# First attention of a two-layer kernel: keys placed alike in every tile, one weight tile a head, weights broadcast from SBUF to SBUF

## The chip, the core and the metric

One core of a Trainium2 chip runs the whole program in one launch. The metric is the device time in microseconds (us). The engines are named as in the profile: PE is the matmul engine (PEld its weight loads), DVE the vector engine, ACT the scalar engine, POOL GpSimd, SP the sync engine, which here only issues DMAs (its queue is SPq).

## The reference, cut to what matters

Two batches of 1,024 tokens go through a layer 0 (attention, then a soft mixture of experts) and a layer 1 (causal attention, then a routed one). Only layer 0's attention is touched. It has 16 query heads over 4 groups of keys and values, head size 64, and its softmax runs in each chunk of 64 keys apart:

```
kc = k.reshape(B, NH, C, SPLIT, HD)        # C = 16 chunks of SPLIT = 64 keys
vc = v.reshape(B, NH, C, SPLIT, HD)
scores = jnp.einsum('bhqd,bhckd->bhcqk', q, kc) * scale
w = jax.nn.softmax(scores.astype(jnp.float32), axis=-1).astype(q.dtype)
chunk_out = jnp.einsum('bhcqk,bhckd->bhcqd', w, vc)
sum_w = w.sum(axis=-1, keepdims=True)
combined = (chunk_out * sum_w).sum(axis=2)
total = sum_w.sum(axis=2)
out = combined / (total + 1e-09)
```

So each exponential is multiplied by a weight that depends on its query and on its key's chunk: 16 x 1,024 weights a head.

## The kernel before, in words

Each engine has its program written out by hand; within a batch the 16 heads are unrolled, and a hardware loop runs over the two batches. Semaphores alone tie the engines together. The batch's attention of layer 0 lasts from about 22 to 534 us, the second one from about 1,105 to 1,620 us.

Queries, keys and values are projected from `att_in` (128 features x 1,024 tokens) by `project_q` (L677), `project_k` (L682) and `project_v` (L688). Tile t holds keys 128t to 128t+127, so it holds chunks 2t and 2t+1: partitions 0 to 63 are one chunk, 64 to 127 the other.

For head i, in `head0(i)`, PE goes through eight steps t:

- `scores(i, t)` (L771, L776): the scores of key tile t against all queries, in two parts (high and low halves of fp32 numbers), 128 keys x 1,024 queries. ACT takes the exponential into `EE` (L1502).
- `maxima(i + 1, ...)` (L750): scores of the next head, queries on partitions, 512 keys at once; DVE reduces each to 8 chunk maxima `mx` (L1919). PE may be only two of these ahead of DVE (banks 5 and 6). They are transposed at the head's end (`turn_maxima`, L757) and are needed by the next head's scores.
- `values0` (L814) of the heads before, two tiles at every odd t, once DVE has multiplied `EE` by the weights (`weigh`, L1948).
- at t = 3 and 5 one projection for the next group (`project_next`).
- at t = 1 `turn_normalisers(i - 1)` (L803).

After the eight steps come `chunk_sums(i)` (L786), the next-but-one head's first two maxima, and `turn_sums(i)` (L796).

The weights of head i are made in this chain: `chunk_sums` sums `EE` over each chunk by a matmul with a 0/1 matrix, four column tiles of 32 at once, 16 matmuls of 512 columns (fp32, so each is two passes in the trace: 32 records a head); ACT copies the sums to `S_sb` (L1482, 128 x 512); `turn_sums` turns them by four transposes; DVE's `normaliser` and `normaliser_parts` (L1928 to L1940) work on 128 numbers a partition; `turn_normalisers` turns them back by four transposes; ACT copies them to `r_rows` (L1477, 128 x 512). Then SP writes four pieces of 16 KB to the DRAM tensor `weight_rows` (`weight_rows_out`, L503), waits for them, and fetches for each key tile two rows, each broadcast over 64 partitions, into a ring of four tiles that lies in `V1` (`weight_tiles_in`, L515: 16 DMAs of 256 KB a head). Each tile's refill waits until DVE has used the tile four before it (`p3_mul`). DVE weighs head i's tiles 0 to 3 at t = 5 and 7 of head i+1, and tiles 4 to 7 at t = 1 and 3 of head i+2.

After head 15 there are no scores: DVE makes head 15's normalisers, weighs tiles 4 to 7 of head 14 and the eight of head 15, and PE does the last values with the output projection (L881) between them.

Of the kernel before, what the change touches and what calls it, by code (L numbers as in the profile page):

```python
# [12 lines left out]
AX = mybir.AxisListType.X  # L13
ds = bass.ds


P = 128
# [18 lines left out]
CQ = NC // 2  # L36
# [3 lines left out]
              "eps_row": NT, "chunk": 4 * 32}  # L40
# [26 lines left out]
def layer_program(nc, A, out, sorted_in, sorted_out, weight_rows):  # L67
    ctx = ExitStack()
    with ctx:
# [16 lines left out]
        chunk_sum = const("chunk").rearrange("p (a c) -> p a c", a=4)  # L86
# [53 lines left out]
        weight_ring = [v[:, :, :].rearrange("p t d -> p (t d)").rearrange("p (o q) -> p o q", o=2) for v in V1]  # L140
# [15 lines left out]
        S_sb = own0[:, 2 * BANK:3 * BANK]  # L156
        r0 = sb("r0", [P, 4, 4, CQ])
        sw = sb("sw", [P, 4, 4, CQ])
        r1 = sb("r1", [P, 4, 4, CQ])
        tot = sb("tot", [P, 4, 2])  # L160
        rp = sb("rp", [P, 4, 4, 32])
        r_rows = sb("r_rows", [P, BANK])
# [200 lines left out]
        wr_in = sem("wr_in")  # L363
        wt_in = [sem(f"wt_in{i}") for i in range(4)]
# [84 lines left out]
        def _(sp):  # L449
# [33 lines left out]
            with sp.Fori(0, NB) as b:  # L483
                for L in range(2):
                    if L == 0:
# [11 lines left out]
                        def weight_rows_out(i):  # L497

                            sp.wait_ge(s_rr, b * HEADS + i + 1)
                            sp.sem_inc(s_held, 1)  # L500
                            for j in range(4):
                                half, odd = divmod(j, 2)
                                sp.dma_start(weight_rows[i % 2, odd * CQ:(odd + 1) * CQ, half * BANK:(half + 1) * BANK],  # L503
                                             r_rows[32 * j:32 * j + CQ, :]).then_inc(wr_in, 16)

                        def weight_tiles_in(i, a):

                            for odd in range(2):
                                t = 2 * a + odd
                                if i >= 1 or t >= 4:  # L510
                                    sp.wait_ge(p3_mul, 1 + (b * HEADS + i) * NT + t - 3)
                                    sp.sem_inc(s_held, 1)
# [8 lines left out]
                        for i in range(HEADS):  # L521
                            weight_rows_out(i)
                            sp.wait_ge(wr_in, (b * HEADS + i + 1) * 64)
                            sp.sem_inc(s_held, 1)
                            for a in range(4):
                                if a == 3 and i % GH == GH - 1 and i // GH + 2 < GROUPS:
                                    next_group(i // GH + 2)
                                weight_tiles_in(i, a)
# [102 lines left out]
        def _(pe):  # L631
# [31 lines left out]
            def attention0(b):  # L663
# [3 lines left out]
                krows = HD + NC  # L667
                h0 = b * HEADS
# [68 lines left out]
                def maxima(i, units):  # L737
# [3 lines left out]
                    for x in units:  # L741
# [8 lines left out]
                        pe.matmul(banks(5 + x % 2, BANK), Q_HIGH[u][:, t * P:(t + 1) * P], KA[g % 2][:, half * BANK:(half + 1) * BANK],  # L750
# [29 lines left out]
                def chunk_sums(i, a):  # L780

                    pe.wait_ge(s["p2_exp"], 1 + (h0 + i) * NT + 2 * a + 2)
                    for half in range(2):
                        for odd in range(2):
# [4 lines left out]
                    if a == 3:  # L789
# [9 lines left out]
                def turn_normalisers(i):  # L799

                    pe.wait_ge(rp_out, h0 + i + 1)
                    for k in range(4):
# [17 lines left out]
                def head0(i):  # L820
# [20 lines left out]
                    for a in range(4):  # L841
                        chunk_sums(i, a)
# [552 lines left out]
        def _(act):  # L1395
# [36 lines left out]
            def attention0(b):  # L1432
# [12 lines left out]
                def high_k(g, half, bank):  # L1445

                    act.wait_ge(s["proj_k"], 1 + 2 * (g0 + g) + half + 1)
                    act.activation(KA[g % 2][:, half * BANK:(half + 1) * BANK], banks(bank, BANK),
# [23 lines left out]
                def normalisers(i):  # L1472

                    act.wait_ge(rb_ps, h0 + i + 1)
                    if i >= 1:
                        act.wait_ge(wr_in, (h0 + i) * 64)
                    act.activation(r_rows[:, :], banks(4, BANK), ACT.Copy).then_inc(s_rr, 1)  # L1477
# [1107 lines left out]
```

## Time and profile before

| | |
|---|---|
| median of 3 runs | 2207.07 us (2201.11 to 2214.0) |
| the profiled execution's own time | 2210.59 us |
| its span, first to last instruction | 2208.5 us |
| PE busy | 1976.8 us, 90% of the span |
| DVE busy | 1440.1 us, 65% |
| ACT busy | 980.7 us, 44% |
| moved by DMA | 187.99 MB |

The span is the profiled execution seen from its first instruction to its last; 2.1 us of its time lie outside. PE's busy time counts matmuls that overlap once.

### The profile page before, as it was taken

The page shows a single profiled execution, that of the slowest core. Times are in us where ns is not written, and L with a number is a line of the kernel's source. Part 1 is how long each engine was busy: PE and PEld are TensorE (multiplying, and loading weights), DVE is VectorE, ACT ScalarE, POOL GpSimd, SP SyncE. Part 2 cuts the span into 40 slices and gives each one's busy share as a digit, 9 for nine tenths or more (in the row PEclk, how much of TensorE's full clock was granted, in tenths as well). Part 3 has the DMA queues.
Part 4 walks back from the last instruction along what each step waited for, and adds up shares of the span by engine and source line. Part 5 has one row for each costly group of instructions (what it writes and reads, how often), then busy time and mean ns, then how long its engine had stood idle before and what let it go on. Part 6 is the DMA issues. An engine that isn't in the chain of part 4 may idle for free.

```text
span 2208.5 us, 32078 instructions
## 1 busy us (share of the span) xinstructions
PE 1976.8 (90%) x10106; PEld 1193.3 (54%) x10106; DVE 1440.1 (65%) x2492; ACT 980.7 (44%) x1377; POOL 586.5 (27%) x549
## 2 busy tenths in 40 slices
PE   6899999996997999998888999999979889999985
PEld 4444444444784655556644444444448755655554
DVE  7677788865327777753467887778561377777443
ACT  3444454441224666662334444444413246656422
POOL 0000000000101798884120000000010047897921
PEclk7999999998887999998879999999979879999987
DMA  2366665567000000000516565656750000000024
GB/s 94 84 154 160 155 149 141 139 161 237 24 1 10 2 10 6 1 1 30 163 39 154 141 146 141 146 141 151 182 198 1 1 10 10 1 6 1 1 79 135
DMA packets 84846, 187.99 MB, mean 85 GB/s; under 512 B 17697, under 2 KB 46754, under 8 KB 83106
## 3 DMA queue, kind: packets, MB, share of 16 engines
q1 hardware_dynamic: 83650, 183.76, 32.8%
q0 software_dynamic: 1024, 2.10, 0.3%
q8 instruction: 88, 1.44, 0.3%
q14 instruction: 84, 0.69, 0.1%
HBM read 178.47 MB, written 8.91 MB: 85 GB/s over the span
## 4 chain that ended last, share of the span: by engine, by line
PE 67%; DVE 14%; issue 9%; ACT 3%; DMA 3%; POOL 2%; SPq 1%; DVEq 0%; another core or an unknown queue 0%; POOLq 0%; ACTq 0%
PE PS L814 10%; PE PS L786 5%; PE PS L750 5%; PE PS L986 4%; PE PS L926 4%; PE PS L966 3%; DVE mx L1919 3%; PE PS L881 3%; PE PS L969 3%; PE PS L1159 3%; PE PS L771 3%; PE PS L776 3%; PE PS L1218 2%; DMA V<-weight_rows 2%; POOL Esum L2463 2%
## 5 line engine op out<-in xcount | busy, mean ns | idle before, releaser
L1919 DVE TENSOR_REDUCE mx<-PS 128x8 f32<-128x512 f32 x512 | 329.6, 686 | 178.7 <-PE PS L750 164.0
L2463 POOL TENSOR_TENSOR Esum<-Esum,EE 128x512 f32<-128x512 f32 (+3 forms) x320 | 341.3, 1094 | 15.5 <-POOL Esum L2463 10.5
L1948 DVE TENSOR_TENSOR EE<-EE,V 128x1024 f32<-128x1024 f32 x256 | 303.1, 1219 | 45.3 <-DMA V<-weight_rows 44.7
L1502 ACT ACTIVATE EE<-PS 128x1024 f32<-128x1024 f32 x256 | 259.9, 1024 | 142.7 <-PE PS L776 141.2
L2052 DVE TENSOR_REDUCE mrow<-PS 128x1 f32<-128x512 f32 (+3 forms) x384 | 204.1, 552 | 99.1 <-PE PS L929 69.9
L2405 POOL TENSOR_TENSOR QA<-hT,QA 128x512 fp32r<-128x512 f32 x2 | 2.6, 1282 | 996.5 <-ACT hT L1690 996.5
L814 PE MATMUL PS<-EE,Vlater 128*64 128x512 f32 x1024 | 250.5, 609 | 9.4 <-ACT U L1468 8.3
L750 PE MATMUL PS<-KA,QA 128*128 128x512 f32 x512 | 204.1, 454 | 31.8 <-DVE mx L1919 25.8
L1586 ACT ACTIVATE EE<-PS 128x1024 f32<-128x1024 f32 (+2 forms) x192 | 138.1, 739 | 121.4 <-PE PS L969 118.7
L771 PE MATMUL PS<-QA,KA 128*128 128x512 f32 x512 | 185.1, 443 | 0.0
L750 PEld LDWEIGHTS PS<-KA,QA 128*128 128x128 f32 x512 | 97.8, 196 | 130.3 <-DVE mx L1919 88.4
L776 PE MATMUL PS<-QB,KB 80*128 80x512 f32 x512 | 163.1, 400 | 0.0
L986 PE MATMUL PS<-EE,V 128*64 128x512 f32 (+3 forms) x640 | 131.2, 522 | 0.0
L2077 DVE COPY_PREDICATED EE<-consts,F 128x256 f32<-128x256 int32 x96 | 95.3, 992 | 47.9 <-ACT EE L1586 47.8
L814 PEld LDWEIGHTS PS<-EE,Vlater 128*64 128x64 f32 x1024 | 61.8, 136 | 115.3 <-issue 92.4
L786 PE MATMUL PS<-EE,consts 128*32 128x512 f32 x1024 | 116.5, 595 | 0.8 <-DVE QA L1896 0.8
L771 PEld LDWEIGHTS PS<-QA,KA 128*128 128x128 f32 x512 | 91.9, 192 | 42.6 <-issue 26.8
L776 PEld LDWEIGHTS PS<-QB,KB 80*128 80x128 f32 x512 | 98.1, 192 | 22.3
L926 PE MATMUL PS<-KA,QA 128*128 128x512 f32 (+1 forms) x192 | 91.1, 475 | 19.2 <-DVE mrow L2052 12.3
L2454 POOL TENSOR_TENSOR Esum<-F,consts 128x1024 f32<-128x1024 f32 x32 | 62.2, 1965 | 93.5 <-PE PS L1010 62.4
L926 PE MATMUL PS<-KC,QC 128*128 128x512 f32 (+1 forms) x192 | 84.4, 440 | 0.6
L926 PEld LDWEIGHTS PS<-KA,QA 128*128 128x128 f32 x192 | 38.3, 199 | 72.4 <-DVE mrow L2052 50.1
(321 smaller groups left out, 3373.6 us busy)
## 6 DMA issues: line engine op xcount, KB each, us to landing
V<-weight_rows SPq DMA_DIRECT2D x512, 256.0 KB, 5.4
EE<-in_w SPq DMA_DIRECT2D x48, 192.0 KB, 2.7
V<-in_Wg SPq DMA_DIRECT2D x4, 1024.0 KB, 6.4
EE<-in_Wu SPq DMA_DIRECT2D x4, 1024.0 KB, 11.8
EE<-in_Wd SPq DMA_DIRECT2D x4, 1024.0 KB, 13.5
sorted_out<-U SPq DMA_DIRECT2D x12, 256.0 KB, 3.1
wo<-in_wo SPq DMA_DIRECT2D x5, 512.0 KB, 4.4
wq_s<-in_wq SPq DMA_DIRECT2D x17, 128.0 KB, 2.8
```

Of the source, the lines that this page charges most:

```text
L750: pe.matmul(banks(5 + x % 2, BANK), Q_HIGH[u][:, t * P:(t + 1) * P], KA[g % 2][:, half * BANK:(half + 1) * BANK], start=True, stop=True).t ...
L771: pe.matmul(banks(own, hi - lo, lo), KA[g % 2][:, t * P:(t + 1) * P], Q_HIGH[u][:, lo:hi], start=True, stop=False)
L776: mm = pe.matmul(banks(own, hi - lo, lo), KB[g % 2][0:krows, t * P:(t + 1) * P], Q_LOW[u][0:krows, lo:hi], start=False, stop=True)
L786: mm = pe.matmul(PS[32 * j:32 * j + 32, 4 * BANK:5 * BANK], chunk_sum[:, a, :], EE[i % 2][:, 2 * a + odd, half * BANK:(half + 1) * BANK], ...
L814: mm = pe.matmul(PS[HD * half:HD * half + HD, 7 * BANK:8 * BANK], V0[i // GH % 2][:, t, :], EE[i % 2][:, t, half * BANK:(half + 1) * BANK] ...
L926: mm = pe.matmul(banks(4 + h, hi - lo), M1[h][p % 2][:, t * P:(t + 1) * P], S1[h][p % 2][:, lo:hi], start=True, stop=not own)
L986: mm = pe.matmul(PS[HD * h:HD * h + HD, 6 * BANK + lo:6 * BANK + hi], V1[g % 2][:, t, at:at + HD], e_tile(t)[:, h, lo - t * P:hi - t * P], ...
L1502: act.activation(EE[i % 2][:, t, :], banks(2 * (t % 2)), ACT.Exp, scale=QSCALE).then_inc(s["p2_exp"], 1)
L1919: dve.tensor_reduce(mx[:, t, half * 8:half * 8 + 8], banks(5 + x % 2, BANK).rearrange("p (c k) -> p c k", c=8), AX, ALU.max).then_inc(s["p ...
L1948: dve.tensor_tensor(EE[i % 2][:, t, :], EE[i % 2][:, t, :], weight_ring[a % 2][:, odd, :], ALU.mult).then_inc(p3_mul, 1)
L2052: dve.tensor_reduce(mrow1[:, h, t, half:half + 1], banks(4 + h, width), AX, ALU.max).then_inc(s["mx_red"], 1)
L2463: ins = pool.tensor_tensor(Esum[:, h, lo:hi], Esum[:, h, lo:hi], e_tile(t)[:, h, lo - t * P:hi - t * P], ALU.add)
```

## The change

Key k*8 + t now sits in tile t at partition k. So partition p of every tile belongs to chunk p // 8, and one 128 x 1,024 tile of weights serves all eight tiles of a head. What follows from it:

- `project_k` and `project_v` read `att_in` through the view `by_place`, that is with a step of eight fp32 elements (32 bytes) between neighbours; V as the stationary operand, K as the moving one. The copies of K are written in runs of 64.
- `maxima` takes 64 keys of each of the eight tiles, so its moving operand is eight runs of 64; DVE's reduction (now L1912) takes for each chunk eight runs of eight columns of PSUM, where it took 64 neighbours.
- `chunk_sums` has the same 0/1 matrix for all tiles. Each key tile needs four matmuls of 256 columns: 32 matmuls of 256 a head (64 records), where there were 16 of 512.
- All 16 chunk rows of a quarter of the queries lie together, so `S_sb`, the transposed sums and `r_rows` are 256 columns wide, and `turn_sums` and `turn_normalisers` need two transposes each. The normalisers are still 128 numbers a partition.
- SP issues four DMAs a head, from `r_rows` straight into one of two tiles in `V1`, each of 128 KB, repeating each of 16 source rows over 8 partitions. There is no DRAM scratch, no wait for it, and no ring. `weigh` waits for all four.

```diff
-                        def weight_rows_out(i):
+                        def weights_in(i):
                             sp.wait_ge(s_rr, b * HEADS + i + 1)
                             sp.sem_inc(s_held, 1)
+                            if i >= 2:
+                                sp.wait_ge(p3_mul, 1 + (b * HEADS + i - 1) * NT)
+                                sp.sem_inc(s_held, 1)
                             for j in range(4):
-                                half, odd = divmod(j, 2)
-                                sp.dma_start(weight_rows[i % 2, odd * CQ:(odd + 1) * CQ, half * BANK:(half + 1) * BANK],
-                                             r_rows[32 * j:32 * j + CQ, :]).then_inc(wr_in, 16)
-                        def weight_tiles_in(i, a):
...
-                                for k in range(2):
-                                    row = weight_rows[i % 2, odd * CQ + 2 * a + k, :]
-                                    sp.dma_start(weight_ring[a % 2][HD * k:HD * k + HD, odd, :],
-                                                 row.partition_broadcast(HD)).then_inc(wt_in[t % 4], 16)
+                                rows = r_rows[32 * j:32 * j + NC, :]
+                                sp.dma_start(weights[i % 2][:, j * QUARTER:(j + 1) * QUARTER],
+                                             rows.unsqueeze(1).to_broadcast([NC, CP, QUARTER])).then_inc(wt_in, 16)
...
+                by_place = x_in[:, :].rearrange("p (k t) -> p t k", t=NT)
...
-                    pe.matmul(banks(bank, BANK), wk_s[:, 0, :], x_in[:, half * BANK:(half + 1) * BANK],
+                    pe.matmul(banks(bank, BANK), wk_s[:, 0, :], by_place[:, :, half * HD:(half + 1) * HD],
...
-                        mm = pe.matmul(banks(bank, HD, t * HD), x_in[:, t * P:(t + 1) * P], wv_s[:, 0:HD],
+                        mm = pe.matmul(banks(bank, HD, t * HD), by_place[:, t, :], wv_s[:, 0:HD],
...
-                        pe.matmul(banks(5 + x % 2, BANK), Q_HIGH[u][:, t * P:(t + 1) * P], KA[g % 2][:, half * BANK:(half + 1) * BANK],
+                        keys = KA[g % 2][:, :].rearrange("p (t k) -> p t k", t=NT)[:, :, half * HD:(half + 1) * HD]
+                        pe.matmul(banks(5 + x % 2, BANK), Q_HIGH[u][:, t * P:(t + 1) * P], keys,
...
-                def chunk_sums(i, a):
-                    pe.wait_ge(s["p2_exp"], 1 + (h0 + i) * NT + 2 * a + 2)
-                    for half in range(2):
-                        for odd in range(2):
-                            j = 2 * half + odd
-                            mm = pe.matmul(PS[32 * j:32 * j + 32, 4 * BANK:5 * BANK], chunk_sum[:, a, :],
-                                           EE[i % 2][:, 2 * a + odd, half * BANK:(half + 1) * BANK],
-                                           start=(a == 0), stop=(a == 3))
+                def chunk_sums(i, t):
+                    pe.wait_ge(s["p2_exp"], 1 + (h0 + i) * NT + t + 1)
+                    for j in range(4):
+                        mm = pe.matmul(PS[32 * j:32 * j + 32, 4 * BANK:4 * BANK + QUARTER], chunk_sum,
+                                       EE[i % 2][:, t, j * QUARTER:(j + 1) * QUARTER], start=(t == 0), stop=(t == NT - 1))
...
                     pe.wait_ge(rp_out, h0 + i + 1)
-                    for k in range(4):
+                    for k in range(2):
                         mm = pe.transpose(banks(4, P, k * P), rp[:, k, :, :].rearrange("p j c -> p (j c)"), ident)
...
-                    act.activation(r_rows[:, :], banks(4, BANK), ACT.Copy).then_inc(s_rr, 1)
+                    act.activation(r_rows[:, :], banks(4, QUARTER), ACT.Copy).then_inc(s_rr, 1)
...
                         dve.tensor_reduce(mx[:, t, half * 8:half * 8 + 8],
-                                          banks(5 + x % 2, BANK).rearrange("p (c k) -> p c k", c=8),
-                                          AX, ALU.max).then_inc(s["p1_max"], 1)
+                                          banks(5 + x % 2, BANK).rearrange("p (t c k) -> p c t k", t=NT, k=CP),
+                                          AXY, ALU.max).then_inc(s["p1_max"], 1)
...
-                    dve.wait_ge(wt_in[t % 4], ((h0 + i) * 2 + t // 4 + 1) * 32)
-                    dve.tensor_tensor(EE[i % 2][:, t, :], EE[i % 2][:, t, :], weight_ring[a % 2][:, odd, :],
-                                      ALU.mult).then_inc(p3_mul, 1)
+                    dve.wait_ge(wt_in, (h0 + i + 1) * 64)
+                    dve.tensor_tensor(EE[i % 2][:, t, :], EE[i % 2][:, t, :], weights[i % 2], ALU.mult).then_inc(p3_mul, 1)
```

PE's program at the end of a head, the last part of `chunk_sums`, the two maxima and `turn_sums`, before (`PS` is PSUM, `Vlater` holds `S_sb`):

```order
L782 REGISTER_ALU
L786 MATMUL PS<-EE,consts 32x512 [waits p2_exp_0]
L786 MATMUL PS<-EE,consts 32x512 x3
L750 MATMUL PS<-KA,QA 128x512 [waits m_rows_0,k_lo_0,q_lo_0]
L750 MATMUL PS<-KA,QA 128x512
L796 MATMUL PS<-consts,Vlater 128x128 [waits s_copy]
L796 MATMUL PS<-consts,Vlater 128x128 x3
```

And the same place in the changed program (line numbers are the changed kernel's):

```order
L772 REGISTER_ALU
L774 MATMUL PS<-EE,consts 32x256 [waits p2_exp_0]
L774 MATMUL PS<-EE,consts 32x256 x3
L740 MATMUL PS<-KA,QA 128x512 [waits m_rows_0,k_lo_0,q_lo_0]
L740 MATMUL PS<-KA,QA 128x512
L783 MATMUL PS<-consts,Vlater 128x128 [waits s_copy]
L783 MATMUL PS<-consts,Vlater 128x128
```

Nothing changed places: four matmuls of 512 columns became four of 256 (there are eight such groups a head now, four before, each with its wait on the exponentials), and four transposes became two; the same halving stands at L803.

SP's program for one head before (`V` is the ring in `V1`), from the rows' way out to the first refills:

```order
L503 DMA weight_rows<-r_rows 8x512 [waits s_rr]
L503 DMA weight_rows<-r_rows 8x512 x3
L523 REGISTER_ALU
L511 ISA [waits wr_in]
L515 DMA V<-weight_rows 64x1024 [waits p3_mul]
L515 DMA V<-weight_rows 64x1024
```

And SP's whole program for two heads after:

```order
L503 ISA [waits s_rr]
L507 DMA V<-r_rows 128x1x256 [waits p3_mul]
L507 DMA V<-r_rows 128x1x256 x3
L500 REGISTER_ALU
L503 ISA [waits s_rr]
L507 DMA V<-r_rows 128x1x256 [waits p3_mul]
L507 DMA V<-r_rows 128x1x256 x3
```

The 20 DMAs of a head became four, and between the normalisers' copy and the weights' issue no wait is left but that for the tile's last use, two heads ago.

## Rows read from the trace of the kernel before

**Rows 1.** Busy time by stretch: us, busy PE, PEld, DVE, ACT, POOL, clock, DMA
```profile
22.60:24.60 2.00, 2.00 (x3) 0.97 (x4) 1.41 (x6) 0.09 (x1) 0.00 (x0) 0.50 0.22 88
66.00:474.00 408.00, 384.42 (x1868) 193.23 (x1872) 320.66 (x485) 194.00 (x243) 0.00 (x0) 1.00 0.61 145
509.60:531.00 21.40, 21.10 (x144) 14.65 (x144) 10.94 (x9) 2.38 (x4) 0.00 (x0) 1.00 0.80 187
```

**Rows 2.** Waits of the whole span: who for whom, total us, times, longest
```profile
DVE EE L1948 <- DMA V<-weight_rows: 44.7, 34, 5.5
```

**Rows 3.** Chain that ended last, 230 to 330 us: start, us, what
```profile
252.63 0.47 PE PS L771 x2
...
257.55 1.93 PE PS L688 x16
...
270.08 3.57 PE PS L786 x32
...
278.59 0.51 PE PS L750
...
280.96 0.59 PE PS L803 x4
...
299.83 3.57 PE PS L786 x32
...
322.18 1.06 PE PS L682 x2
```

**Rows 4.** Timeline of the same stretch: start, us, what, idle time before it
```profile
252.75 0.60 ACT L1477 ACTIVATE r_rows<-PS 128x512 f32<-128x512 f32 x1 [3.26 <-PE PS L803]
...
263.34 2.35 DVE L1948 TENSOR_TENSOR EE<-EE,V 128x1024 f32<-128x1024 f32 x2
...
270.47 0.13 PEld L786 LDWEIGHTS PS<-EE,consts 128*32 128x32 f32 x4 [0.30 <-issue]
...
276.31 0.29 DVE L1929 TENSOR_TENSOR sw<-PS,r 128x128 f32<-128x128 f32 x1
...
276.84 0.28 DVE L1931 TENSOR_TENSOR r<-sw,r 128x128 f32<-128x128 f32 x1
...
277.99 1.10 PE L750 MATMUL PS<-KA,QA 128*128 128x512 f32 x2 [0.65 <-DVE mx L1919]
```

**Rows 5.** Costliest groups: busy, mean ns of one, idle time before
```profile
L1502 ACT ACTIVATE EE<-PS 128x1024 f32<-128x1024 f32 x256 | 259.9, 1024 | 142.7 <-PE PS L776 141.2
```

**Rows 6.** Timeline of the first batch's head 1
```profile
76.11 0.60 ACT L1477 ACTIVATE r_rows<-PS 128x512 f32<-128x512 f32 x1 [1.51 <-PE PS L803]
...
84.91 1.22 DVE L1948 TENSOR_TENSOR EE<-EE,V 128x1024 f32<-128x1024 f32 x1 [0.66 <-DMA V<-weight_rows]
...
87.18 1.22 DVE L1948 TENSOR_TENSOR EE<-EE,V 128x1024 f32<-128x1024 f32 x1 [1.05 <-DMA V<-weight_rows]
...
89.66 1.04 PE L757 MATMUL PS<-consts,mx 128*16 128x128 f32 x8 [3.11 <-DVE mx L1919]
```

**Rows 7.** Timeline of the start of head 15
```profile
477.81 0.66 PE L796 MATMUL PS<-consts,Vlater 128*128 128x128 f32 x4 [0.72 <-ACT Vlater L1482]
```

**Rows 8.** Timeline of the attention's end, after head 15
```profile
499.47 0.60 ACT L1482 ACTIVATE Vlater<-PS 128x512 f32<-128x512 f32 x1 [4.58 <-PE PS L786]
...
505.96 2.50 DVE L1948 TENSOR_TENSOR EE<-EE,V 128x1024 f32<-128x1024 f32 x2 [0.31 <-DMA V<-weight_rows]
...
509.53 5.62 PE L881 MATMUL PS<-wo,U 128*128 128x128 f32 x48
...
512.14 1.22 DVE L1948 TENSOR_TENSOR EE<-EE,V 128x1024 f32<-128x1024 f32 x1 [3.68 <-DMA V<-weight_rows]
```

**Rows 9.** DMA issues: size of one, median us from issue to landing
```profile
V<-weight_rows SPq DMA_DIRECT2D x512, 256.0 KB, 5.4
...
wq_s<-in_wq SPq DMA_DIRECT2D x17, 128.0 KB, 2.8
```

**Rows 10.** Chain that ended last, at the first group's projections
```profile
22.56 2.07 PE PS L682 x2
```

More of the change, by code:

```diff
@@ L13 @@
 AX = mybir.AxisListType.X
+AXY = mybir.AxisListType.XY
 ds = bass.ds
@@ L35 @@
 EPS_TOTAL = 1e-9
-CQ = NC // 2
+CP = CHUNK // NT
+QUARTER = T // 4
 CONST_COLS = {"ident": 128, "neg": 128, "mask": 128, "first": 16, "after": NT,
-              "eps_row": NT, "chunk": 4 * 32}
+              "eps_row": NT, "chunk": P}
 CONST_AT = {}
@@ L64, with layer_program @@
 ROUTE_COLS = {"before": P, "ones": P, "upto": E1 * E1, "many": NT, "at": TILES1}
-def layer_program(nc, A, out, sorted_in, sorted_out, weight_rows):
+def layer_program(nc, A, out, sorted_in, sorted_out):
     ctx = ExitStack()
@@ L85, in layer_program @@
         neg_fr = sb("neg_fr", [P, P], FR)
-        chunk_sum = const("chunk").rearrange("p (a c) -> p a c", a=4)
+        chunk_sum = const("chunk")[:, 0:32]
         ones_row = sb("ones_row", [1, P])
@@ L139, in layer_program @@
         Vlater = sb("Vlater", [P, NT - 2, 2, P])
-        weight_ring = [v[:, :, :].rearrange("p t d -> p (t d)").rearrange("p (o q) -> p o q", o=2) for v in V1]
+        weights = [V1[0][:, 4 * i:4 * i + 4, :].rearrange("p t d -> p (t d)") for i in range(2)]
         own0 = Vlater[:, :, :, :].rearrange("p t h d -> p (t h d)")
@@ L154, in layer_program @@
         mx1 = sb("mx1", [P, NT, 33])
[L156 to L162, printed above, removed]
+        S_sb = own0[:, 2 * BANK:2 * BANK + QUARTER]
+        r0 = sb("r0", [P, 2, 4, NC])
+        sw = sb("sw", [P, 2, 4, NC])
+        r1 = sb("r1", [P, 2, 4, NC])
+        tot = sb("tot", [P, 2, 4])
+        rp = sb("rp", [P, 2, 4, 32])
+        r_rows = sb("r_rows", [P, QUARTER])
         with nc.sbuf_tensor("QA2", [P, T], FR) as QA2, nc.sbuf_tensor("QB2", [P, T], FR) as QB2, \
@@ L362, in layer_program @@
         s_rr = sem("s_rr")
-        wr_in = sem("wr_in")
-        wt_in = [sem(f"wt_in{i}") for i in range(4)]
+        wt_in = sem("wt_in")
         p3_mul = sem("p3_mul")
@@ L521, in _ @@
                         for i in range(HEADS):
[L522 to L528, printed above, removed]
+                            weights_in(i)
+                            if i % GH == GH - 1 and i // GH + 2 < GROUPS:
+                                next_group(i // GH + 2)
                     else:
@@ L778, in scores @@
                     mm.then_inc(s["p2_full"], 1)
[L780 to L789 removed]
+                def chunk_sums(i, t):
[3 more added lines that the diff above has]
+                                       EE[i % 2][:, t, j * QUARTER:(j + 1) * QUARTER], start=(t == 0), stop=(t == NT - 1))
+                    if t == NT - 1:
                         mm.then_inc(s_full, 1)
@@ L801, in turn_normalisers @@
                     pe.wait_ge(rp_out, h0 + i + 1)
-                    for k in range(4):
+                    for k in range(2):
                         mm = pe.transpose(banks(4, P, k * P), rp[:, k, :, :].rearrange("p j c -> p (j c)"), ident)
@@ L840, in head0 @@
                     bank_four_free(i)
-                    for a in range(4):
-                        chunk_sums(i, a)
+                    for t in range(NT):
+                        chunk_sums(i, t)
                     if i + 2 < HEADS:
@@ L1447, in high_k @@
                     act.wait_ge(s["proj_k"], 1 + 2 * (g0 + g) + half + 1)
-                    act.activation(KA[g % 2][:, half * BANK:(half + 1) * BANK], banks(bank, BANK),
+                    keys = KA[g % 2][:, :].rearrange("p (t k) -> p t k", t=NT)[:, :, half * HD:(half + 1) * HD]
+                    act.activation(keys, banks(bank, BANK).rearrange("p (t k) -> p t k", t=NT),
                                    ACT.Copy).then_inc(s["k_hi"], 1)
@@ L1797, in row_under_k, with first_chunk_under_k @@
                                   ALU.mult, ALU.add)
+            def first_chunk_under_k(h, lo, hi, value):
+                row = KB[h][HD:HD + 1, :].rearrange("p (t k) -> p t k", t=NT)[:, :, lo:hi]
+                dve.tensor_scalar(row, consts[HD:HD + 1, lo:hi].unsqueeze(1).to_broadcast([1, NT, hi - lo]), 0.0, value, ALU.mult, ALU.add)
             def modulation():
@@ L1901, in low_k @@
                     dve.wait_ge(s["k_hi"], 1 + 2 * (g0 + g) + half + 1)
-                    cols = slice(half * BANK, (half + 1) * BANK)
-                    dve.tensor_tensor(KB[g % 2][0:HD, cols], banks(bank, BANK, rows=HD), KA[g % 2][0:HD, cols],
+                    low, high = [k[g % 2][0:HD, :].rearrange("p (t k) -> p t k", t=NT)[:, :, half * HD:(half + 1) * HD]
+                                 for k in (KB, KA)]
+                    dve.tensor_tensor(low, banks(bank, BANK, rows=HD).rearrange("p (t k) -> p t k", t=NT), high,
                                       ALU.subtract).then_inc(s["k_lo"], 1)
@@ L2504, in const_array @@
     put("eps_row", rows)
-    a = np.arange(4)[None, :, None]
-    col = np.arange(32)[None, None, :]
-    put("chunk", (col == 2 * a + (np.arange(P) // CHUNK)[:, None, None]).reshape(P, 4 * 32))
+    put("chunk", q == p // CP)
     k = np.arange(T)[None, :]
-    own_chunk = ((p - HD) == k // CHUNK).astype(np.float32)
+    own_chunk = ((p - HD) == k % P // CP).astype(np.float32)
     return c, own_chunk
@@ L2580 @@
     sorted_out = nc.dram_tensor("sorted_out", (TILES1 * P, P), F32, kind="Internal").ap()
-    weight_rows = nc.dram_tensor("weight_rows", (2, 2 * CQ, T), F32, kind="Internal").ap()
-    layer_program(nc, A, out, sorted_in, sorted_out, weight_rows)
+    layer_program(nc, A, out, sorted_in, sorted_out)
     r = _run(nc, [arrays], core_ids=[0])
```

24 lines of the change are left out of this document (9 added, 15 removed).

## The prediction

> **What bounds the kernel now.** I read the page's busy times first: in the steady part of the first attention PE is busy 384 of 408 us, DVE 321, at PE's full clock [rows 1]. So 24 us of PE idleness are shared by some 14 heads. Then I took the chain that ended last through one head (29.75 us from one `chunk_sums` to the next): nearly all of it is PE working without a gap. One stretch is different: between 270.08 + 3.57 = 273.65 us, when PE turns to the first two maxima for DVE, and 278.59, the chain is DVE's (two reductions, four normaliser steps, two reductions), and PE, limited to two maxima ahead, sits idle 0.65 us before one and again before the next [rows 3, 4]. What is cut from PE's work inside that stretch buys nothing; what is cut on PE elsewhere buys its full time.
>
> Then the waits for the weights' DMA. In all 34 waits cost DVE 44.7 us [rows 2], which looks like the prize of the change. But where do they lie? In the steady head DVE starts weighing at 263.34 with no wait; `r_rows` was copied by 252.75 + 0.60 = 253.35, so the weights have 10.0 us there [rows 4]. The waits lie in head 1 of each batch [rows 6] and after the maxima are over, in head 15 and behind it [rows 8]. Behind it, DVE waits 3.68 us for head 15's first tile, but PE is at work on the output projection from 509.53 on [rows 8], and from 509.6 to 531 PE is busy 21.1 of 21.4 us [rows 1]. So most of those 44.7 us are waits of an engine that nobody waits for.
>
> **The change part by part.**
>
> *Normalisers' transposes (L803).* Four take 0.59 us on the chain in every head [rows 3], two will take 0.30. They stand behind L814, outside DVE's stretch, so 0.29 us are saved in heads 1 to 15 of both batches: 30 x 0.29 = 8.8 us. The last head's own pair stands beside DVE's weighing and is counted at nothing.
>
> *Sums' transposes (L796) and the two copies.* In the steady head L796 lies inside DVE's stretch: nothing, and the two copies by ACT, 0.2 us shorter each, lie beside PE's work. It is different where there are no more maxima, at the start of head 15 and after it: there PE or DVE waits for copy and transposes in turn. The copy takes 0.60 us for 512 columns; with 1,024 in 1.024 us [rows 5], a column costs 0.83 ns, so 256 fewer save 0.21. L796 takes 0.66 for four [rows 7] and saves 0.30. That is 0.5 us at both places [rows 7, 8], 1.0 a batch, 2.0 in all.
>
> *The weights' way.* In head 1 the waits of 0.66 and 1.05 us stand before DVE's next maxima, for which PE then waits 3.11 us [rows 6]: 1.7 us a batch, if the new way is faster. After head 15 a wait of 0.31 stands before PE's last values of head 14 [rows 8]. Together 2.0 a batch, 4.0 in all. Is it faster? The nearest row for a DMA of 128 KB lands 2.8 us after its issue, one tile DMA of 256 KB after 5.4 [rows 9]. From below: four issued behind each other, all landed some 4 us after the copy. From above: four that don't overlap, 4 x 2.8 = 11.2 us. I take about 5, since the 512 KB are what two of today's 16 tile DMAs carry. That is in time for head 1, whose first weighing starts at 84.91, 8.2 us after the copy [rows 6]. In the steady head anything up to 10.0 us is hidden behind PE's and DVE's other work; if that cover went, DVE's weighing would push the maxima behind it (a rival below). The DRAM write, its wait and the ring go away on SP alone. SP's new wait on `p3_mul` is for a tile used two heads ago, done at t = 3 of the head before the one in which it is asked; queued behind it are only the next group's projection weights, which have heads of time.
>
> *Chunk sums (L786).* 32 records of 512 columns take 3.57 us [rows 3], 0.446 a group of four. 64 of 256 stream as many columns. What could be added is the overhead of a group. The weight loads of a group of four take 0.13 us [rows 4] while the group before streams, and a group will stream for 0.22, so they stay covered. I take 0; from above, if loads and matmuls came in turn, 0.13 + 0.22 = 0.35 a group, 5.6 us a head.
>
> *Reduction over chunks in pieces (L1919).* As many elements. The nearest row: a DVE step over runs of 8 in PSUM takes 0.29 us, one over dense SBUF data of the same size 0.28 [rows 4]. That is at most 0.01 us for 16 runs, so 0.04 for 64. About five reductions a head are on the chain: 0 to 6 us in all. I take 0. The maxima's matmul reads its keys in runs of 64; I take 0 there too.
>
> *Strided projections (L682, L688).* K and V are projected from `att_in` with a step of 32 bytes. No row of this trace has a PE operand with such a step. From below: nothing. From above, every such instruction twice as long, as K's two are at half the clock (2.07 us at clock 0.50 [rows 1, 10], against 1.06 [rows 3]). A group costs 2 x 1.06 + 1.93 = 4.05 us [rows 3] in the heads that project it, all on the chain. With three groups a batch that is 24.3 us, with the first group's K some 3 more: 27 us. Today these fp32 matmuls take 0.53 us for 512 columns, where the fp32r ones of the scores take 0.23 (0.47 for two [rows 3]). So they ask for an element only half as often as PE is able to read, which leaves room for a slower read. I take 0, and hold this for the least certain choice.
>
> The Trainium skill speaks against that choice. SBUF — State Buffer, section "Door 1: The DMA port swizzle", says that SBUF is read in lines of 16 bytes, that at least two hits a line are needed for full bandwidth, and that fp32 strides are free up to four elements; this step is eight. By that rule the projections would be slower, and the result is the first rival's; no row of the trace shows it.
>
> Sum: 8.8 + 2.0 + 4.0 = 14.8 us saved of the profiled 2210.6, hence 2195.8, 0.67% less. The median of the runs shown is 2207.07, so 2207.07 x 2195.8 / 2210.6 = 2192.3.
>
> **The rivals.** My forecast, 14.8 saved, has 0.52.
>
> 1. *The strided reads cost.* For it: eight elements' step, 4 groups, both operands. Against: these matmuls already ask at half the rate. If both kinds double, 27 - 15 = +12 us, 2219: slower by a little over half a per cent (chance 0.15). If only the loads or only the moving operand suffer, +13 to +15 eat the gain: 2206 (0.13).
>
> 2. *Weights too late, slower.* One mechanism: the four DMAs read only 16 partitions each, eight times over, and come one after another. It decides from 10.0 us after the copy on. At 11.2 DVE weighs 1.2 us late, before the two reductions whose maxima PE must turn at the head's end; PE waits that long in some 28 heads, +34 us, less the 9 to 11 that the rest saves: about 2231 (0.05).
>
> 3. *Loads not hidden in the chunk sums.* +2.0 us in each of 32 heads, +65 - 15: 2257. For it: twice as many loads under matmuls half as long. Against: 0.13 is below 0.22 (0.06).
>
> 4. *DVE's reduction is clearly slower in pieces*, say 0.1 us and more an instruction: five on the chain in 30 heads, +15 and up, and DVE, busy 321 of 408 us, would come near PE: 2207 and up, mostly slower (0.06). Against: the runs of 8 above.
>
> 5. *The change gives nothing* (PE's shorter work is lost in waits for DVE or ACT further on): 2205 (0.03).
>
> **How the numbers follow.** The likeliest case has a range of its own: with 6 us for the reductions and 2 for the chunk sums 2200, with a little more from head 1 and the end 2188. The overall range reaches down to 2186 for the spread of the runs and up to 2222 to take in the strided reads in full; it leaves out rivals 2, 3 and part of 4. A measurement of this kernel can tell about 0.5%, 11 us, from no change. Faster by more: the forecast's case but for 0.06 of it, its weak end, 0.46. Slower: 0.15 + 0.05 + 0.06 and 0.05 of rival 4, 0.31. Within: 0.06 + 0.13 + 0.01 + 0.03, 0.23.
>
> **What would show it.** In the changed profile: two transposes in 0.30 us on the chain at each head's t = 1; no wait of DVE's for the weights in head 1; `chunk_sums` at 3.5 to 3.7 us a head; reductions at 686 ns; K's projection at 1.06 us a half and V's at 1.93 a group, the numbers on which it would fail first; a head's length shorter by 0.3 us. The end from 509 to 531 us must stay as long as it is, since PE fills it. The prediction is wrong if a head is longer than now: at K's and V's heads alone it is rival 1, in all heads rivals 2 to 4, told apart by whether DVE waits for a DMA, PE's loads idle, or the reduction's mean grew.

## The result, and the profile after

| | before | after |
|---|---|---|
| median | 2206.93 us, 6 runs (2201.11 to 2214.0) | 2222.26 us, 6 runs (2219.14 to 2227.78) |
| ratio after to before | | 1.0076, 95% interval 1.0059 to 1.0093 |
| span of the profiled execution | 2208.5 us | 2220.4 us |

The changed kernel is 15.3 us slower. I had forecast 2192 us, with a range of 2186 to 2222: the sign was wrong. I had given a slower kernel a chance of 0.31.

The page of the changed kernel, busy time by engine, DMA, the costliest groups (as in [rows 2, 5]) and the DMA issues [rows 9]:

```profile
PE 1986.3 (89%) x11002; PEld 1226.6 (55%) x11002; DVE 1434.2 (65%) x2488; ACT 968.1 (44%) x1377; POOL 586.5 (26%) x549
...
DMA packets 60269, 68.48 MB, mean 31 GB/s; under 512 B 10529, under 2 KB 55970, under 8 KB 58530
...
L1912 DVE TENSOR_REDUCE mx<-PS 128x8 f32<-128x512 f32 x512 | 329.4, 685 | 204.2 <-PE PS L740 193.3
L1940 DVE TENSOR_TENSOR EE<-EE,V 128x1024 f32<-128x1024 f32 x256 | 300.0, 1217 | 15.3 <-DMA V<-r_rows 14.9
L774 PE MATMUL PS<-EE,consts 128*32 128x256 f32 x2048 | 117.1, 381 | 0.8 <-DVE QA L1888 0.8
...
V<-r_rows SPq DMA_DIRECT2D x128, 128.0 KB, 3.8
```

Read alone, these rows look like success: DMA moves 68 MB where it moved 188, DVE waits 14.9 us for the weights where it waited 44.7 [rows 2], and the reduction over eight pieces takes 685 ns, as long as the one over neighbours (686). The chain that ended last says where the time went instead. Two heads of it, one that projects V for the next group and one that doesn't, then the next one's K:

```profile
243.80 3.59 PE PS L774 x64
...
254.69 0.37 PE PS L790 x2
...
255.53 0.47 PE PS L766 x2
...
260.00 3.95 PE PS L677 x16
...
264.54 0.85 PE PS L766 x2
265.39 0.85 PE PS L740 x2
...
275.86 3.59 PE PS L774 x64
...
305.42 3.59 PE PS L774 x64
...
321.62 2.01 PE PS L671 x2
```

V's 16 instructions (L677) take 3.95 us where they took 1.93, a half of K (L671) 2.01 where it took 1.06, the sums (L774) 3.59 where they took 3.57, and the normalisers' two transposes (L790) 0.37 where four took 0.59 [rows 3]. A head without K or V lasts 305.42 - 275.86 = 29.56 us, where it was 299.83 - 270.08 = 29.75 [rows 3]. The head with V lasts 32.06.

And there is something that no rival had. Behind V's projection the same two score matmuls take 0.85 us that took 0.47 just before. Busy times and granted clock (the column with 1.00 and 0.51) around it:

```profile
260.00:264.00 4.00, 4.00 (x17) 4.00 (x18) 1.22 (x2) 0.02 (x1) 0.00 (x0) 1.00 0.31 43
264.20:267.60 3.40, 3.40 (x10) 2.64 (x9) 1.29 (x2) 1.40 (x2) 0.00 (x0) 0.51 0.00 0
```

For 3.4 us right behind V's projection the clock was at the lower of its two levels (1.2 instead of 2.4 GHz). The changed kernel has three such stretches, at 264.2, 1233.6 and 1476.0 us, each in one of the six heads that project V. The heads with V that have none last 30.7 to 30.8 us, so one costs about 1.3.

What a chain cannot show is how these add up. I therefore cut both attentions at fixed instructions (the first projection of K, the first `chunk_sums`, the next one, that of head 15, and the attention's first residual step). Sums over both batches, in us:

| | K0 to first sums | head 1 | heads 2 to 15 | end | both attentions |
|---|---|---|---|---|---|
| before | 92.3 | 54.3 | 803.2 | 76.7 | 1026.5 |
| after | 93.8 | 50.4 | 821.5 | 75.9 | 1041.6 |

The 15.1 us of this table are all of the loss: the heads 2 to 15 lose 18.3, head 1 wins 3.9. Of head 1's 3.9, 1.6 are the kernel before's own bad luck: at 90.8 us, in its first batch, it had the lower clock for 3.4 us, and that head lasted 27.94 us where the second batch's lasted 26.35. Outside the attentions the two profiles differ by 3 us, the other way.

### The profile page after: what moved, and what is told of

Same layout as the page of the kernel before. It is cut to its first block, busy times and chain, and to the rows that moved or that the text cites. A ratio compares the mean times of both kernels' runs of the same rounds, so it can differ in the third digit from the quotient of the medians.

```text
span 2220.4 us, 32848 instructions
## 1 busy us (share of the span) xinstructions
PE 1986.3 (89%) x11002; PEld 1226.6 (55%) x11002; DVE 1434.2 (65%) x2488; ACT 968.1 (44%) x1377; POOL 586.5 (26%) x549
## 3 DMA queue, kind: packets, MB, share of 16 engines
q0 software_dynamic: 1024, 2.10, 0.3%
## 4 chain that ended last, share of the span: by engine, by line
PE 68%; DVE 16%; issue 9%; ACT 3%; POOL 2%; DMA 0%; DVEq 0%; SPq 0%; another core or an unknown queue 0%; POOLq 0%; ACTq 0%
PE PS L801 10%; PE PS L774 5%; PE PS L740 5%; DVE mx L1912 4%; PE PS L973 4%; PE PS L913 4%; PE PS L953 3%; PE PS L868 3%; PE PS L761 3%; PE PS L766 3%; PE PS L956 3%; PE PS L1146 3%; PE PS L1205 2%; POOL Esum L2453 2%; DVE EE L1940 2%
## 5 line engine op out<-in xcount | busy, mean ns | idle before, releaser
L1912 DVE TENSOR_REDUCE mx<-PS 128x8 f32<-128x512 f32 x512 | 329.4, 685 | 204.2 <-PE PS L740 193.3
L1940 DVE TENSOR_TENSOR EE<-EE,V 128x1024 f32<-128x1024 f32 x256 | 300.0, 1217 | 15.3 <-DMA V<-r_rows 14.9
L761 PE MATMUL PS<-QA,KA 128*128 128x512 f32 x512 | 192.7, 458 | 0.0
L740 PEld LDWEIGHTS PS<-KA,QA 128*128 128x128 f32 x512 | 99.2, 199 | 130.2 <-DVE mx L1912 96.1
L2068 DVE COPY_PREDICATED EE<-consts,F 128x256 f32<-128x256 int32 x96 | 92.5, 963 | 50.5 <-ACT EE L1574 50.4
L774 PE MATMUL PS<-EE,consts 128*32 128x256 f32 x2048 | 117.1, 381 | 0.8 <-DVE QA L1888 0.8
L913 PE MATMUL PS<-KA,QA 128*128 128x512 f32 (+1 forms) x192 | 90.0, 469 | 19.2 <-DVE mrow L2043 12.1
L774 PEld LDWEIGHTS PS<-EE,consts 128*32 128x32 f32 x2048 | 63.3, 110 | 64.2 <-issue 24.3
## 6 DMA issues: line engine op xcount, KB each, us to landing
EE<-in_Wu SPq DMA_DIRECT2D x4, 1024.0 KB, 11.2
```

The costliest lines, as they stand in the source:

```text
L761: pe.matmul(banks(own, hi - lo, lo), KA[g % 2][:, t * P:(t + 1) * P], Q_HIGH[u][:, lo:hi], start=True, stop=False)
L774: mm = pe.matmul(PS[32 * j:32 * j + 32, 4 * BANK:4 * BANK + QUARTER], chunk_sum, EE[i % 2][:, t, j * QUARTER:(j + 1) * QUARTER], start=(t ...
L913: mm = pe.matmul(banks(4 + h, hi - lo), M1[h][p % 2][:, t * P:(t + 1) * P], S1[h][p % 2][:, lo:hi], start=True, stop=not own)
L1912: dve.tensor_reduce(mx[:, t, half * 8:half * 8 + 8], banks(5 + x % 2, BANK).rearrange("p (t c k) -> p c t k", t=NT, k=CP), AXY, ALU.max).t ...
L1940: dve.tensor_tensor(EE[i % 2][:, t, :], EE[i % 2][:, t, :], weights[i % 2], ALU.mult).then_inc(p3_mul, 1)
```

## The experiments

My theory: the new step of `att_in` doubles the work of K's and V's projections (a K half from 1.06 to 2.01 us, a V group from 1.93 to 3.95, together 3.9 us a group) and, behind V's, brings the clock down, while all else of the change saves what I had forecast. Rivals: the loss comes from another part of the new placement (sums in pieces, keys in runs), or the step matters only together with the rest of the change, or the weights' DMAs are behind it.

**Both projections dense, in the changed kernel.** K and V are taken from neighbouring columns, so keys stand in the wrong places and the output is not the reference's; the instructions are otherwise the same.

```diff
-  ... wk_s[:, 0, :], by_place[:, :, half * HD:(half + 1) * HD]
+  ... wk_s[:, 0, :], x_in[:, half * BANK:(half + 1) * BANK]
-  ... by_place[:, t, :], wv_s[:, 0:HD]
+  ... x_in[:, t * P:(t + 1) * P], wv_s[:, 0:HD]
```

> The changed kernel (2222 us), but K and V are projected from 512 and 128 neighbouring columns of att_in, without the step of eight elements; keys and values then belong to other places than the weights assume, everything else is as in the change. Theory (the strided PE reads are the loss): in heads that project for the next group K's halves go from 2.01 back to 1.06 us and V from 3.95 to 1.93, 6 x (1.9 + 2.0) = 23.5 us, some 2 more at the first group, and three dips of the clock behind V's projection (1.3 us each) go too: about 2193, faster than before. Rival (the loss lies in the new placing itself: maxima in runs of 64, more chunk sums, or in the DMAs): the stride gives back little, 2212 to 2222.

Measured: 2185.99 us (2176.25 to 2191.07), ratio to before 0.9914 (0.9885 to 0.9943). Both attentions take 1009.8 us, 31.8 less than in the changed kernel. I compare attentions because the rest isn't steady: behind the second attention, in code that no edit touches, this profile is 7.9 us shorter than that of before. The same place of its chain, with no slow clock behind V:

```profile
252.50 1.93 PE PS L677 x16
...
254.95 0.47 PE PS L766 x2
...
265.05 3.59 PE PS L774 x64
...
275.93 0.37 PE PS L790 x2
...
294.58 3.59 PE PS L774 x64
...
310.76 1.06 PE PS L671 x2
```

**The step alone, in the kernel before.** The reverse edit; the output is again not the reference's.

```diff
+                by_place = x_in[:, :].rearrange("p (k t) -> p t k", t=NT)
-  ... x_in[:, half * BANK:(half + 1) * BANK]        # K
+  ... by_place[:, :, half * HD:(half + 1) * HD]
-  ... x_in[:, t * P:(t + 1) * P]                    # V
+  ... by_place[:, t, :]
```

> The kernel before (2207 us), only with K and V projected through the step of eight elements; keys and values end up at other places than their chunks. Theory: +23.5 us in the heads, +2 to 3 at the first group, up to 5 for dips of the clock: 2231 to 2238. Rival (the old kernel hides it, or the loss belongs to other parts of the change): 2207 to 2215.

Measured: 2230.41 us (2217.55 to 2237.75), ratio 1.0125 (1.0080 to 1.0171). Both attentions take 1053.5 us, 27.0 more than before. So the step costs this in the old kernel too, without any of the rest.

**Only one of the two strided.** First V dense and K strided, then K dense and V strided (either half of the first edit).

> The changed kernel with only V projected from neighbouring columns (values don't match their keys then). Theory: 6 x 2.0 = 12 us, and if V's slow weight loads are what lets the clock fall, the dips of 1.3 us each go as well: 2206. If the dips come from elsewhere: 2210, with dips left.

> The changed kernel with only K projected from neighbouring columns. Theory: 6 x 1.9 = 11.4 us and about 2 at the first group: 2209, dips of the clock behind V's projection still there. Rival (V's loads alone carry the loss, K's slower matmuls being made good by less waiting for DVE): 2218 to 2222.

Measured: with K strided alone 2202.66 us (2199.34 to 2206.18), ratio 0.9999 (0.9988 to 1.0011); with V strided alone 2212.01 (2199.45 to 2218.32), ratio 1.0038 (1.0009 to 1.0066). The attentions take 1019.3 and 1034.4 us, so against the dense 1009.8 K's step costs 9.5 and V's 24.6: more than twice as much, though on the chain a group's K and V grow alike (2 x 0.95 and 2.02 us). By the table's columns, K's 9.5 are 0.6, 2.0, 7.9 and -1.0 (head 1 hides half of its K), V's 24.6 are 3.6, 0.0, 20.0 and 1.0. The medians give 16.7 for K and 26.0 for V, with the unsteady rest in them. The durations of the two lines (minimum, median and maximum ns), first with only K strided:

```profile
L671 PE MATMUL PS<-att_in,wk_s x32: 1076/1098/1261, 22.7 to 1403.6; 128*128 128x512 f32 x32
...
L677 PEld LDWEIGHTS PS<-wv_s,att_in x128: 186/192/210, 28.0 to 1457.7; 128*128 128x128 f32 x128
L677 PE MATMUL PS<-wv_s,att_in x128: 238/275/323, 28.9 to 1457.7; 128*128 128x64 f32 x128
```

And with only V strided:

```profile
L671 PE MATMUL PS<-att_in,wk_s x32: 590/593/1217, 24.1 to 1415.9; 128*128 128x512 f32 x32
...
L677 PEld LDWEIGHTS PS<-wv_s,att_in x128: 312/335/338, 29.5 to 1471.4; 128*128 128x128 f32 x128
L677 PE MATMUL PS<-wv_s,att_in x128: 219/401/451, 29.9 to 1471.5; 128*128 128x64 f32 x128
```

An instruction whose moving operand has a step takes 1.85 times as long, the load of a stationary one 1.75 times. The slow clock goes with V's loads: the run with only K strided has none in its heads 2 to 15, the one with only V strided has four, one of them beginning while V's group was still running (257.88 to 261.88 us):

```profile
256.90:260.80 3.90, 3.90 (x19) 3.09 (x15) 2.21 (x2) 0.00 (x0) 0.00 (x0) 1.00 0.55 85
260.80:267.60 6.80, 6.80 (x19) 4.92 (x20) 2.17 (x4) 2.65 (x3) 0.00 (x0) 0.50 0.01 2
```

Its slow stretches last 6.8, 3.4, 6.8 and 3.4 us; at 1.3 us for 3.4 they cost 7.7 by this estimate, and 6 groups x 2.02 = 12.1 us are the loads themselves, together 19.8 of the 20.0 us that heads 2 to 15 lose against the dense run.

**How large a step.** Steps of four and of two elements (16 and 8 bytes) instead of eight; same sizes, wrong keys. One run each, so what counts is how long these instructions take.

```diff
-  ... by_place[:, :, half * HD:(half + 1) * HD]
+  ... x_in[:, half * BANK:(half + 1) * BANK].rearrange("p (k s) -> p s k", s=4)   # or s=2; V likewise
```

> The changed kernel with K and V projected through a step of four fp32 elements (16 bytes) in place of eight; keys and values then belong to other places. What is read is the duration of these instructions. By the Trainium skill, SBUF, section on the DMA port swizzle, four fp32 elements are still free: K at 0.59 us a record and V's loads at 192 ns, as dense. Rival: each element lies in a line of its own already, so it costs as much as eight: 1.10 us and 335 ns. Or the step's length matters gradually: between.

> The same with a step of two elements (8 bytes): two of the elements wanted lie in one line of 16 bytes. If the line is what counts, dense durations (0.59 us, 192 ns). If any step other than one costs, 1.10 us and 335 ns.

Measured: 2224.4 us with a step of four, 2194.4 with two; both attentions 1041.6 and 1012.5 us. The lines with four, then with two:

```profile
L671 PE MATMUL PS<-att_in,wk_s x32: 1058/1081/1242, 23.3 to 1423.2; 128*128 128x512 f32 x32
...
L677 PEld LDWEIGHTS PS<-wv_s,att_in x128: 307/330/330, 28.9 to 1479.1; 128*128 128x128 f32 x128
```

```profile
L671 PE MATMUL PS<-att_in,wk_s x32: 610/612/1217, 23.6 to 1395.1; 128*128 128x512 f32 x32
...
L677 PEld LDWEIGHTS PS<-wv_s,att_in x128: 192/196/197, 28.8 to 1448.8; 128*128 128x128 f32 x128
```

So four costs what eight does (1081 and 1100 ns) and two next to nothing (612 against 594 when dense). The Trainium skill, SBUF — State Buffer, section "Door 1: The DMA port swizzle", gives two statements: at least two hits in a 16-byte line are needed for full bandwidth, and fp32 strides are free up to four elements. The runs agree with the first (two elements, two hits a line: 612 ns) and contradict the second: with four elements only one hit falls into a line, and that takes 1081 ns.

**The weights' DMAs.** First each of the four DMAs is issued twice, the second time into an unused part of `V1`, and all eight are waited for, by DVE and by ACT before it overwrites `r_rows`. Second, the rows go through DRAM again, with four pieces out, a wait, and four broadcasts in; all else as changed.

```diff
+   sp.dma_start(spare[:, j * QUARTER:(j + 1) * QUARTER],
+                rows.unsqueeze(1).to_broadcast([NC, CP, QUARTER])).then_inc(wt_in, 16)
-   dve.wait_ge(wt_in, (h0 + i + 1) * 64)
+   dve.wait_ge(wt_in, (h0 + i + 1) * 128)
```

> The changed kernel with each of the four weight DMAs of a head issued a second time, into an unused tile; DVE waits for all eight. Theory (the weights' way is hidden in all heads but head 1 and the end of each batch): some 3 us later, so 2222 to 2227. Rival (the weights are only just in time, and part of the loss lies here): DVE waits in each head, 2240 and more.

```diff
+   sp.dma_start(weight_rows[i % 2, j, :, :], r_rows[32 * j:32 * j + NC, :]).then_inc(wr_in, 16)
+   sp.wait_ge(wr_in, (b * HEADS + i + 1) * 64)
...
-   rows = r_rows[32 * j:32 * j + NC, :]
+   rows = weight_rows[i % 2, j, :, :]
```

> The changed kernel with the four pieces of r_rows written to DRAM, waited for, and broadcast from there, one tile a head as in the change: the SBUF-to-SBUF part alone undone. Theory: some 3 us later in head 1 and the end, 2222 to 2228, no wait of DVE's in the other heads. Rival (the gain that the change does have comes from the direct way in all heads): 2235 and more.

Measured: through DRAM 2222.08 us (2219.18 to 2230.95), ratio 1.0068 (1.0043 to 1.0094), the changed kernel's own time, and head 1 as short as there (50.4 us in both batches). So leaving out the DRAM scratch is worth nothing by itself. Head 1's gain comes from something else in the change; fetching 512 KB a head instead of 4 MB is the likely part, but was not tried alone. The broadcasts themselves are even quicker from DRAM: 4.4 us from the first issue to the last one's semaphore (median of 32 heads), where the same sizes from `r_rows` take 6.4. That makes up for 2.0 of the 2.9 us by which the write and its wait put off the first issue. One of them takes 2.5 us in the median, where it takes 3.8 from `r_rows`:

```profile
V<-weight_rows SPq DMA_DIRECT2D x128, 128.0 KB, 2.5
```

The doubled DMAs were a miss for my theory: 2298.05 us (2294.92 to 2302.54), ratio 1.0411 (1.0382 to 1.0440), where I had expected 2222 to 2227. Its waits, and the queue and DVE in one head:

```profile
DVE EE L1943 <- DMA V<-r_rows: 78.2, 26, 9.7
```

```profile
237.12 0.38 ACT L1468 ACTIVATE r_rows<-PS 128x256 f32<-128x256 f32 x1 [3.46 <-PE PS L793]
...
237.76 0.56 SPq L508 DMA_DIRECT2D V<-r_rows  x1
...
242.56 1.38 SPq L510 DMA_DIRECT2D V<-r_rows  x1
...
244.88 1.27 SPq L510 DMA_DIRECT2D V<-r_rows  x1
...
249.71 2.36 DVE L1943 TENSOR_TENSOR EE<-EE,V 128x1024 f32<-128x1024 f32 x2 [1.47 <-DMA V<-r_rows]
```

By the packets' records the last byte lands 6.3 us after the copy's end in the changed kernel (median of 32 heads) and 11.8 with eight DMAs, so the second four add 5.5 us. Each takes 3.8 from issue to landing (median); four thus overlap in part, but their time grows with their number. DVE starts weighing 10.65 us after the copy in most heads without having waited. Only the weights of heads 14 and 15 are late in the changed kernel too: DVE is ready 2.5 and 3.5 us after the copy and waits 4.4 and 3.1, which in two batches is all of its 14.9 us. With eight, DVE waits in 26 places, 63 us more than in the changed kernel, and the attentions grow by 69 us. My expectation had four more DMAs at some 3 us, where they add 5.5, more than the 4.3 us that the changed kernel has to spare in its steady heads.

**A version without the step on the hot path.** GpSimd, idle during the attention, copies `att_in` once a batch into the order by place, into the unused part of `V1`; groups 1 to 3 are projected from this copy, group 0 still from `att_in` with the step. It computes all of the reference. In a second version V of group 0 waits for the copy as well.

```diff
+   pool.tensor_copy(placed, att_in[:, :].rearrange("p (k t) -> p t k", t=NT)).then_inc(xp_in, 1)
...
+   src = placed if g else by_place        # K, and V; in the second version V from placed always
+   if i == 1:
+       pe.wait_ge(xp_in, b + 1)
```

> The change in full, and GpSimd, idle then, copies att_in once a batch into a tile in which the tokens lie by place (1,024 elements, in the unused half of V1); K and V of groups 1 to 3 are projected from it without a step, group 0's as in the change. Same output as the reference. Theory: K at 1.06 us a half and V at 1.93 a group in the heads, no dips of the clock behind them: about 27 us less than the change, 2195, and 0.4 to 0.7% under before. Rival (the copy, whose reads have the step, or its use of the port it shares with DVE costs on the path): 2200 to 2210.

> As the one before, and group 0's V is projected from the copy too, for which PE waits at the start of each batch. Theory: V's strided loads at the start cost about 1.8 us a batch, so 2 to 4 us less than the one before, if the copy is done by then. Rival (the copy takes longer than the 3 us between att_in and that projection): PE waits, and it is equal or slower.

Measured: 2190.47 us (2179.28 to 2199.82), ratio to before 0.9926 (0.9903 to 0.9948), faster than both kernels; the second version 2198.12 (2190.18 to 2209.88), ratio 0.9955 (0.9933 to 0.9977). The first one's copy and the lines of groups 1 to 3:

```profile
L2397 POOL COPY V<-att_in x2: 2034/2058/2081, 24.3 to 1110.6; 128x1024 f32<-128x1024 f32 x2
```

```profile
L674 PE MATMUL PS<-V,wk_s x24: 590/592/697, 83.6 to 1390.9; 128*128 128x512 f32 x24
```

```profile
L681 PEld LDWEIGHTS PS<-wv_s,V x96: 186/192/192, 141.1 to 1444.5; 128*128 128x128 f32 x96
```

Its attentions take 1015.4 us, 11.2 less than before, with no slow clock in heads 1 to 15. The other 8 us of the 19.3 between the medians are then outside the attentions, mostly in code that the edit doesn't touch. In the profiles this code varies by more than that: between the attentions it took 561.1 us here at a mean granted clock of 0.92, and 571.4 at 0.90 in the kernel before; behind the second one 577.0 at 0.91, and 588.0 at 0.89 (580.1 at 0.90 in the dense run). So the lower clock may well be all of the 8 us; whether the copy has a part in that, the runs don't show. The second version wins 3.0 us up to the first sums in batch 1, of which V's quicker loads are 1.9 (3.78 to 1.9 us) and the lower clock, here for 17.1 instead of 23.9 us, may be the rest. It loses 13.3 in batch 2, in one wait:

```profile
PE PS L681 <- POOL V L2398: 13.2, 1, 13.2
```

In batch 2 GpSimd is still busy with the last additions of the layer before when K of group 0 is projected, and comes to the copy only at 1107.39 us.

## Why the prediction was wrong

**The step that failed: "Strided projections (L682, L688) ... I take 0".** The step costs 31.8 us in the changed kernel and 27.0 in the kernel before. My argument for nothing was that these fp32 matmuls ask for an element only half as often as PE is able to read, "which leaves room for a slower read". It was a guess about a rate, not a row: K's matmuls went from 593 to 1100 ns. It also said nothing about V, whose strided operand is loaded, not streamed, and whose rows gave no hint of room. The Trainium skill's statement on 16-byte lines (SBUF — State Buffer, section "Door 1: The DMA port swizzle") spoke against me, and the runs agree with its sign; I gave rival 1 in full only 0.15. With two bounds and no row between them I should not have taken the end that the forecast liked.

What the step does is set a pace of its own. The first group's K shows it. Its first half falls into the lower clock (mean granted clock 0.50 from 22.18 to 24.36 us), its second doesn't (1.00):

```profile
22.18 2.18 PE PS L671 x2
...
26.61 1.83 PE PS L671 x2
```

Dense, this first half took 2.07 us [rows 10]. So at the lower clock the step adds 0.11 us to a half, and at the full one 0.8 to 0.95. A half is two matmuls of 512 columns, so with the step that is 1.8 to 2.1 ns an element at either clock, and dense at full clock 1.0 (1.06 us). The room that I had argued with is not there.

**That the kernel before lost just the 27 us of my upper bound is partly luck.** The bound had 24.3 for six groups and "some 3 more" for the first group's K. The six groups' own instructions cost 6 x 3.9 = 23.5 at most, of which head 1's K hides a part. To this come two things that the bound left out: the first group's V (3.60 us on the chain, where the loads and matmuls took 1.9 dense), and the slow clock. In the kernel before six slow stretches, 7.7 us by an estimate of 1.3 each, are in the 27.0, and 1.6 us are off it because head 1 of the kernel before had its own. In the changed kernel, against the dense one, the 31.8 are 5.8 before the first sums, 2.0 in head 1 and 24.0 in heads 2 to 15, 3.9 of these for three slow stretches.

**Rival 1's sum** was 27 - 15 = +12 us, 2219, with the right mechanism; it is 31.8 - 16.7 = +15.1 in the attentions, and 2222.3 was measured.

**The rest of the sum held.** Forecast 14.8 us; the dense run has attentions 16.7 us shorter than before, and its median is 17.5 below that of before. By its terms:

- Normalisers' transposes: forecast 0.29 a head; 0.22 on the chain (0.59 to 0.37), and the plain head is shorter by just this: 29.75 to 29.53 us. Two transposes don't take half of four here. Heads 2 to 15 gained 5.7 us, where I had 28 x 0.29 = 8.1 and 1.0 for head 15's start.
- Head 1: forecast 1.99 a batch; 2.14 in batch 2. In batch 1 it is 3.75, 1.6 of it because the kernel before had the lower clock there for 3.4 us. Its DVE has no wait for the weights there, as forecast:

```profile
78.22 0.38 ACT L1465 ACTIVATE r_rows<-PS 128x256 f32<-128x256 f32 x1 [1.73 <-PE PS L790]
...
87.29 2.34 DVE L1940 TENSOR_TENSOR EE<-EE,V 128x1024 f32<-128x1024 f32 x2
```

- The end: forecast 0.81 a batch; 0.81 in batch 2, and nothing in batch 1, where the dense run had the lower clock for 3.4 us at 496.8. In the version with GpSimd's copy, which has no slow stretch there, it is 0.94 and 0.80. DVE's wait for head 15's weights stayed (in the changed kernel, below), and costs little, because PE is in the output projection, as [rows 8] had it with 3.68:

```profile
516.67 5.62 PE L868 MATMUL PS<-wo,U 128*128 128x128 f32 x48
518.72 9.17 DVE L1940 TENSOR_TENSOR EE<-EE,V 128x1024 f32<-128x1024 f32 x8 [3.12 <-DMA V<-r_rows]
```

- 4.3 us of the 16.7 come from the stretch ahead of the first sums, nearly all of it in batch 2, where I had forecast nothing and the granted clock differs from one execution to the next. They make my sum look better than it was: without them 12.4 stand against 14.8, and with the two slow stretches just named set right (1.6 off, 1.0 on) 11.8.
- Sums of 256 columns: forecast 0, measured 0.02 us a head. Reductions in pieces: forecast 0, the mean went from 686 to 685 ns. Rivals 3, 4 and 5 are out.

**Rival 2** (weights too late) didn't happen, but its mechanism exists, as the doubled DMAs show: time grows with their number, and from 10.65 us after the copy on it decides, where I had 10.0. I was nearly right about this point and lucky about the price, which I took as "about 5" from a row of another shape; it is 6.3.

## What to carry to other kernels

A view that makes neighbours in the output out of far elements in the input isn't free because the instruction count stays: for every PE operand look at the step within a partition, and from four fp32 elements on (three was not tried) reckon with 2 ns an element until a row says otherwise. For these fp32 matmuls that is nearly double; for a matmul that asks faster when dense it may be worse, which no run here tried. When an idle engine can lay the data out once (2.06 us of GpSimd a batch here), the better layout downstream can be had without that price, if nothing on the path has to wait for the copy. And a cost with only two bounds deserves the chance of each bound, above all when one argument of the text speaks for the far one.

## What the runs showed that I had not expected

- The lower clock behind V's strided loads: after one group of 16 loads and matmuls of 3.95 us without an idle gap, the granted clock fell from 1.00 to 0.51 for 3.4 or 6.8 us. It did so in three of six such heads of the changed kernel, in two of the same six by way of DRAM, in two with a step of four, in four with V alone strided, in all six of the kernel before with the step, and in all six with doubled DMAs. In the six profiles with dense or nearly dense loads there (a step of two among them) it did so in none of 36. That it comes with these loads is shown; why, and why not each time, is not. The clock falls elsewhere too: ahead of the kernel before's slow stretch at 90.8 us PE had been busy for 1.6 of 4.7 us.
- Both kinds of operand suffer alike from the step: 593 to 1100 ns moving, 192 to 335 ns stationary. At two elements neither does (612 and 196 ns).
- DMAs that each repeat 16 source partitions eight times move 512 KB in 5.5 us more when four are added, 95 GB/s. From DRAM four of the same size land in 4.4 us instead of 6.4, and the kernel is no slower for the detour.
